# The first attention's values: who measures the rows, and one norm batch instead of three

## What is computed

```
h   = h + attention0(layernorm(h)) @ Wo
xn  = (h - mean(h)) / sqrt(var(h) + 1e-5)            # per row of 256
logits = xn @ router_w ; top 2 of 8 experts per row ; gate = softmax(top 2)
e_out  = layernorm(xn + W2 gelu(W1 xn + b1) + b2)    # each row by its 2 experts
h   = h + sum over the 2 experts of gate * e_out
h   = h + attention1(layernorm(h)) ; h = h + low_rank_ffn(layernorm(h))
```

## Time and profile before

| what | us |
|---|---|
| median of 3 runs (808.05 to 809.29) | 808.77 |
| the profiled execution's own time | 809.9 |
| its span, first to last instruction | 807.9 |
| busy: PE, PEld, DVE, POOL, ACT | 710.4, 608.9, 515.6, 423.8, 378.5 |
| PE's share of the chain that ended last | 74% |

### The profile page before, as it was taken

How to read it: one execution, slowest core, us unless ns; L and a number is a source line. 1 busy time by engine, 2 the same in 40 slices (tenths; PEclk the granted TensorE clock), 3 DMA queues, 4 the chain that set the end, 5 groups by cost and what they waited for, 6 DMA issues and landing times.

```text
span 807.9 us, 13117 instructions
## 1 busy us (share of the span) xinstructions
PE 710.4 (88%) x4247; PEld 608.9 (75%) x4247; DVE 515.6 (64%) x1230; ACT 378.5 (47%) x930; POOL 423.8 (52%) x360
## 2 busy tenths in 40 slices
PE   3669999999999999999847837999999999677797
PEld 3669998989889898655446736999999999444686
DVE  4567888778787787768988881223322233488957
ACT  3346666666576664643131332444444444156232
POOL 5555587676776853447949712343334432136640
PEclk9879999999999999999878967999999999689799
DMA  7943233323333202000011058898999992200001
GB/s 232 255 125 109 69 111 110 113 87 94 105 114 114 59 1 104 1 1 1 0 58 48 27 209 302 332 335 300 334 329 334 325 320 106 109 35 2 0 1 66
DMA packets 47064, 108.58 MB, mean 134 GB/s; under 512 B 5028, under 2 KB 24728, under 8 KB 39576
## 3 DMA queue, kind: packets, MB, share of 16 engines
q1 hardware_dynamic: 44408, 100.68, 37.3%
q0 software_dynamic: 2592, 7.10, 2.4%
HBM read 101.58 MB, written 6.17 MB: 133 GB/s over the span
## 4 chain that ended last, share of the span: by engine, by line
PE 74%; DVE 12%; SPq 3%; DMA 3%; POOL 3%; issue 2%; ACT 2%; DVEq 0%; ACTq 0%; POOLq 0%
PE banks L1703 12%; PE banks L1711 12%; PE banks L291 9%; PE banks L293 9%; PE banks L292 9%; PE banks L298 5%; PE banks L304 4%; PE banks L1311 3%; PE banks L1358 1%; DVE banks L1485 1%; PE banks L1285 1%; DVE a_o L1576 1%; DVE a_prod L1198 1%; PE banks L1341 1%; SPq L386 1%
## 5 line engine op out<-in xcount | busy, mean ns | idle before, releaser
L408 POOL TENSOR_TENSOR x_lo<-xraw,x_hi 128x512 fp32r<-128x512 f32 x81 | 105.6, 1304 | 99.7 <-ACT x_hi L402 99.6
L1794 ACT ACTIVATE hid<-banks,b 128x128 f32<-128x128 f32 x216 | 79.4, 368 | 110.4 <-PE banks L1703 110.4
L291 PE MATMUL banks<-wc_hi,x_hi 128*128 128x256 f32 x324 | 99.1, 306 | 19.4 <-POOL x_hi L411 13.3
L292 PE MATMUL banks<-wc_lo,x_hi 128*128 128x256 f32 x324 | 94.0, 290 | 0.0
L293 PE MATMUL banks<-wc_hi,x_lo 128*128 128x256 f32 x324 | 93.9, 290 | 0.0
L1959 DVE TENSOR_TENSOR res<-banks,xb 128x256 f32<-128x256 f32 x27 | 11.5, 425 | 127.3 <-PE banks L1711 127.3
L291 PEld LDWEIGHTS banks<-wc_hi,x_hi 128*128 128x128 f32 x324 | 64.3, 198 | 21.3 <-issue 13.5
L442 DVE BATCH_NORM_STATS2 stats<-banks 128x6 f32<-128x256 f32 x81 | 34.6, 428 | 69.4 <-ACT pe_sb L436 68.9
L291 PE MATMUL banks<-wkv_hi,xg_hi 128*128 128x512 f32 x162 | 70.9, 438 | 6.5 <-DVE xg_lo L503 6.3
L1832 POOL TENSOR_TENSOR y<-bve,mhalf 128x1 f32<-128x1 f32 x27 | 20.2, 747 | 105.7 <-DVE bve L1967 105.7
L402 ACT ACTIVATE x_hi<-xraw 128x768 fp32r<-128x768 f32 (+1 forms) x81 | 66.8, 830 | 12.1 <-DMA xraw<-in_x_rest 12.1
(11 more groups left out here) (331 smaller groups left out, 1828.1 us busy)
## 6 DMA issues: line engine op xcount, KB each, us to landing
w_raw<-in_w SPq DMA_DIRECT2D x28, 1024.0 KB, 6.6
xraw<-in_x_main SPq DMA_DIRECT2D x27, 768.0 KB
w1more<-in_w SPq DMA_DIRECT2D x13, 1024.0 KB, 6.0
w2more<-in_w SPq DMA_DIRECT2D x13, 1024.0 KB, 8.9
xraw<-in_x_rest SPq DMA_DIRECT2D x48, 96.0 KB
xraw<-in_x_rest SPq DMA_DIRECT2D x27, 114.0 KB
yl<-y_rows SPq DMA_DIRECT2D x2, 1028.0 KB, 6.9
a_w<-in_qkv_w SPq DMA_DIRECT2D x2, 768.0 KB, 5.4
```

The costliest lines, as they stand in the source:

```text
L291: pe.matmul(dst, a[0], b[0], start=start, stop=False)
L292: pe.matmul(dst, a[0], b[1], start=False, stop=False)
L408: pool.tensor_tensor(x_lo[:, i % RING_X, :], xraw[:, k, 0:KF].rearrange("p c b -> p (c b)"), x_hi[:, i % RING_X, 0:KF * P], ALU.subtract). ...
L1794: act.activation(hid[:, s % 2, fc, :], bank(fc % 2, 0, P), ACT.Gelu, bias=b1[:, bass.ds(e * FC + fc, 1)]).then_inc(sem("gelu_made"), 1)
```

## The change

ACT's copy of `h(t)` also accumulates the sum of the row (`accum_out`). A new `square_row(t)` on ACT, one turn behind, makes minus the mean with a one-element copy and then squares the row with that as its bias, accumulating the squared deviations; the squares themselves go to the place of `x2`, where they are overwritten later. DVE's `add_o` is left for layer 1 only. The three norm batches become one: `row_variances` (DVE, between the second and third `route_top`), one `pow` of ten elements a partition on POOL, `row_shifts` (DVE, behind the third `route_top` and ahead of the routing's chain). ACT writes all ten rows of `x2` behind it. `center_router` moves from ahead of DVE's second odd tile to behind the second half of the softmax, ahead of the third. All three `route_top` now stand in `dve_route`. One semaphore of a memset is merged into another.

```diff
 def copy_h(act, layer, t):
-    act.activation(h_at(t), bank(6 + t % 2), ACT.Copy).then_inc(sem("a_h_made"), 1)
+    act.activation(h_at(t), bank(6 + t % 2), ACT.Copy, accum_out=row_sum_of[:, layer, t:t + 1]).then_inc(sem("a_h_made"), 1)
+def square_row(act, t):
+    act.wait_ge(sem("a_h_made"), t + 1)
+    act.activation(mv[1][:, t, 0:1], row_sum_of[:, 0, t:t + 1], ACT.Copy, scale=-1.0 / C).then_inc(sem("row_measured"), 1)
+    act.wait_ge(sem("row_measured"), 2 * t + 1)
+    act.activation(x2[:, t * C:(t + 1) * C], h_at(t), ACT.Square, bias=mv[1][:, t, 0:1],
+                   accum_out=mv[1][:, t, 1:2]).then_inc(sem("row_measured"), 1)
...
 # act_attention, layer 0, turn t, behind copy_hT(t - 3)
-if layer == 0 and t == 7:
-    norm_rows(act, 0)
+if layer == 0 and t:
+    square_row(act, t - 1)
...
 copy_h(act, layer, T - 1)
 if layer == 0:
+    square_row(act, T - 1)
     for t in range(T - 3, T):
         copy_hT(act, t)
...
 # dve_attention
-if layer == 0 and i == 1:
+if layer == 0 and i == 2:
     center_router(dve)
...
+def row_variances(dve):
+    dve.wait_ge(sem("row_measured"), 2 * T)
+    dve.tensor_scalar(veps[1][:, :], mv[1][:, :, 1], 1.0 / C, 1e-5, ALU.mult, ALU.add).then_inc(sem("var_made"), 1)
+def row_shifts(dve):
+    n = batch_of("experts", 0)[0]
+    dve.wait_ge(sem("rstd_made"), n + 1)
+    dve.tensor_tensor(nmr[1][:, :], mv[1][:, :, 0], rstd[1][:, :], ALU.mult).then_inc(sem("nmr_made"), 1)
...
 # dve_route
-for a, b in GROUPS[1:]:
+for a, b in GROUPS:
     route_top(dve, link, a, b)
+    if b == T - 2:
+        row_variances(dve)
+row_shifts(dve)
 link(dve.tensor_copy(topf[:, :, :], topi[:, :, 0:2]))
...
-def norm_rows(act, group):
-    normalized_scales(act, "experts", group)
-    for t in range(*GROUPS[group]):
+def norm_rows(act):
+    normalized_scales(act, "experts")
+    for t in range(T):
         normalize(act, x2[:, t * C:(t + 1) * C], h_at(t), t, 1).then_inc(sem("x2_made"), 1)
```

More of the change, by code:

```diff
@@ L100, in vision_tower @@
         spare = sb("spare", [P, 2])
+        row_sum_of = sb("row_sum_of", [P, 2, T])
         rstd = [sb(f"rstd{i}", [P, T]) for i in range(3)]
@@ L319, in vision_tower @@
         SET = {"class": 1, "attention 0": 2, "experts": 1, "attention 1": 0, "low rank": 1}
-        BEFORE = {"class": 0, "attention 0": 0, "experts": 1, "attention 1": NW, "low rank": 2}
+        BEFORE = {"class": 0, "attention 0": 0, "attention 1": NW, "low rank": 1}
         BATCHES = [("attention 0", 0, NW - 2), ("attention 0", NW - 2, NW - 1), ("attention 0", NW - 1, NW), ("attention 0", NW, T),
-                   ("experts", 0, 4), ("experts", 4, 8), ("experts", 8, T), ("attention 1", 0, 2), ("attention 1", 2, 6), ("attention 1", 6, T),
+                   ("experts", 0, T), ("attention 1", 0, 2), ("attention 1", 2, 6), ("attention 1", 6, T),
                    ("low rank", 0, T - BT), ("low rank", T - BT, T)]
@@ L1269, in pool_attention @@
             if layer == 0:
-                for part in range(3):
-                    inverse_std(pool, *batch_of("experts", part))
+                inverse_std(pool, *batch_of("experts", 0))
             else:
@@ L1577, in dve_attention, with add_o @@
                    .then_inc(sem("a_o_made"), 1)
-                while added < t - 3:
-                    add_o(dve, layer, added)
+                while layer == 1 and added < t - 3:
+                    add_o(dve, added)
                     added += 1
[L1581 to L1593, removed]
+            if layer == 1:
+                for t in range(added, T):
+                    add_o(dve, t)
+        def row_variances(dve):
[5 more added lines that the diff above has]
+            dve.tensor_tensor(nmr[1][:, :], mv[1][:, :, 0], rstd[1][:, :], ALU.mult).then_inc(sem("nmr_made"), 1)
+        def add_o(dve, t):
+            dve.wait_ge(sem("a_h_made"), seen(1, "h_made", t + 1))
+            ends = {7: 0, T - 1: 1}
+            tile_stats(dve, "low rank", t, h_at(t))
             if t in ends:
-                add_eps(dve, following, ends[t])
-            if layer == 0 and t - 1 in ends:
-                shift_of(dve, *batch_of(following, ends[t - 1]))
+                add_eps(dve, "low rank", ends[t])
         def top_two(dve, link, x, t8, ti, tf, count):
@@ L1762, in sp_experts @@
                 load_weights(sp, s, s if s < E else sp.value_load(owner[0:1, s - E:s - E + 1], min_val=0, max_val=E - 1))
-        def norm_rows(act, group):
-            normalized_scales(act, "experts", group)
-            for t in range(*GROUPS[group]):
+        def norm_rows(act):
+            normalized_scales(act, "experts")
+            for t in range(T):
                 normalize(act, x2[:, t * C:(t + 1) * C], h_at(t), t, 1).then_inc(sem("x2_made"), 1)
         def act_experts(act):
-            norm_rows(act, 1)
-            norm_rows(act, 2)
+            norm_rows(act)
             act.wait_ge(sem("tw_made"), 1)
@@ L1807, in pool_route_constants @@
             pool.memset(not_first[:, :, :], 1.0).then_inc(sem("route_fill"), 1)
-            pool.wait_ge(sem("route_fill"), 2)
+            pool.wait_ge(sem("route_fill"), 3)
             pool.affine_select(out=before[:, :], in_=before[:, :], compare_op=ALU.is_gt, fill=0.0,
@@ L1868, in dve_route @@
                .then_inc(sem("route_ready"), 1)
-            shift_of(dve, *batch_of("experts", 2))
             link(dve.tensor_tensor(tw[:, :, :], top[:, :, 0:2], top[:, :, 0:1].broadcast_to([P, T, 2]), ALU.subtract))
@@ L2172, in _ @@
         def _(pool):
-            pool.memset(ident[:, :], 0.0).then_inc(sem("ident_zeroed"), 1)
+            pool.memset(ident[:, :], 0.0).then_inc(sem("route_fill"), 1)
             pool.memset(mhalf[:, :], -0.5).then_inc(sem("consts_made"), 1)
@@ L2176, in _ @@
             pool.memset(xraw[:, :, 4, :], 0.0).then_inc(sem("pads_zeroed"), 1)
-            pool.wait_ge(sem("ident_zeroed"), 1)
+            pool.wait_ge(sem("route_fill"), 1)
             pool.affine_select(out=ident[:, :], in_=ident[:, :], compare_op=ALU.not_equal, fill=1.0,
```

## The result

| | median us | lowest to highest | runs |
|---|---|---|---|
| before, measured beside it | 809.67 | 807.75 to 811.01 | 8 |
| changed | 811.55 | 809.88 to 812.08 | 8 |

The ratio is 1.0026, 95% interval 1.0015 to 1.0038. The changed kernel is slower, by 1.9 us between the medians and by 1.2 to 3.1 us by the interval. The profiled execution took 811.4 with a span of 809.7; before it was 809.9 and 807.9.

A forecast was written before the change was run, and what follows sets the result against it. POOL was taken to pace the values' stage, a PE-ACT zigzag to end it, then DVE's routing chain, and PE from 490 on. Terms -0.05 + 1.3 = +1.25 on 808.77 gave 810.0 us, range 807.8 to 811.8.

The forecast's parts named there:

- DVE's relief: Values' stage: 7.8 us less before DVE's last odd tile, ready near 452 instead of 460; worth nothing.
- ACT's turn: Values' stage: 1.1 us added per tile (read-outs 0.20, copy 0.20, square 0.51), hidden in ACT's idle time in turns 1 to 6.
- The end of the zigzag: End of the values' stage, between PE and ACT: gain spent on the last square; -0.05, bounds -0.3 and +0.5.
- the upper bound: Zigzag's end with a read-out of 0.4: +0.5, from three read-outs less 0.3 of slack, then two more.
- the first rival: Slower: ACT's read-out costs 0.6, hT(7) at 468.06, zigzag +1.25, kernel 811.3; chance 0.17.
- The norm batch: Routing on DVE: topf newly waits for POOL's ten-element pow, 471.72 instead of 470.44; +1.3, bounds 1.1 and 1.6.
- The rows of x2: Behind the shift: ACT's ten rows end at 476.8, SP's weight loads start 4 us later; all hidden, at nothing.
- the second: Faster rival: first gather meets no backlog, lands in 3.2, saves 3.4, kernel 806.7; chance 0.12, half of it a partial form.
- the third: Rival: third route_top's index search waits at the shared port until 471.56; +1.6, kernel 810.4; chance 0.05.
- The read-out of 0.6: The claim of the first rival: ACT's read-out costs more than an instruction; slower from 0.35; chance 0.17.
- DVE as the bound: Fourth rival, values' stage: DVE's end was the bound, -7.8 + 1.3, kernel 802.3; chance 0.03.
- The clock's rise: PE's rise to 2.4 GHz, first expert slot: 0.65 gained if it stays put, 0.65 lost if it comes as much later.

The follow-up runs named there:

- e4: Kernel before with one norm batch of ten rows, x2 written behind all copies, shift behind the scan, DVE still measuring every row; 0.9992 of before's time.
- e8: Changed kernel with the router centred ahead of DVE's second odd tile again and layer 1's copies of h not accumulating; one run, 811.15 us.
- e2: e1 with the last tile's square_row also moved, behind copy_hT(9) instead of ahead of copy_hT(7); 0.9988 of before's time.
- e1: Changed kernel with one line moved, row_shifts behind the routing's scan (rank) instead of ahead of topf; 1.0002 of before's time.
- e3: Changed kernel with the ten-element power done twice on POOL, first to a place nobody reads; 1.0025 of before's time.
- e5: e4 with the loads of b1, b2 and gamma issued ahead of the stores of x2; 0.9987 of before's time.

## Why the prediction was right, and where it was not

The time of 811.55 lies in the range, near its upper end of 811.8; 0.9 of its distance from the forecast 810.0 is that the kernel before, too, came out higher beside it (809.67 and not 808.77). The forecast, +1.25, is at the lower edge of the first interval, +1.2 to +3.1, and below the second, +1.6 to +3.7. I gave "within 0.2%" more chance than "slower", where 0.26% and 0.33% were measured. The mechanism was right and the sum too small.

**DVE's relief worth nothing: right.** e4 leaves every measurement on DVE, e8 undoes the centring, and PE takes DVE's last tile at the same place in both. In the changed kernel that tile is ready at 452.39 on the clock of before (452 forecast). POOL's folds and PE's order set it.

**ACT's turn: right.** Read-out 0.19 for 0.20, copy 0.20, square 0.51; nothing on the path in turns 1 to 6.

**The end of the zigzag: right in kind, -0.21 for -0.05.** `turn_h(8)` is 0.21 sooner. I had put `h(9)`'s read-out behind its copy and `copy_hT(7)` behind the last read-out; the trace has each overlap by 0.1. e2 shows the square's own price there, 0.84. The working of the upper bound does not add up: it names three read-outs ahead of `h(9)`, but the +0.5, and the 468.06 of the first rival, count two. With three the bound is +0.65. At the measured read-out of 0.19 nothing hangs on it.

**The norm batch: right.** `veps` at 469.29 on the clock of before (469.36 forecast), the power 1.97 (1.95), `topf` at 471.71 (471.72). The parts are right to 0.1; that the end is right to 0.01 is chance. Taken away in e1 and doubled in e3, the wait answered each time.

**The sum's missing parts.** Two terms stood nowhere. Layer 1's `copy_h` got the read-out as well, 0.1 at each of two places on the path: I priced the edit in layer 0 only, though the diff shows `layer` in its index. And from `topf` to `dst_row` 0.44 was added: PE's two rank products took 0.56 and 0.57, 0.36 and 0.37 before, with PE at its lower level (granted clock 0.50; 1.00 before). When I wrote down what e1 would show, I held a longer idle time of PE for the cause, but e4 has the same 2.36 of idle time as the kernel before and still 0.56 and 0.57. The rows of PE, before and in e4:
```profile
471.81 0.36 PE L1677 MATMUL banks<-rank,before 128*128 128x8 f32 x2 [2.36 <-DVE rank L1866]
```
```profile
471.06 0.56 PE L1672 MATMUL banks<-rank,before 128*128 128x8 f32 x2 [2.36 <-DVE rank L1860]
```
Of all the traces, only that of the kernel before has these products at the upper level. So 0.4 of the 1.71 may belong to that execution and not to the change; whether it does stays open, as there is one trace of it. Without it the terms give 1.5, with it 1.9.

**The rows of x2 hidden: right, but narrowly.** The loads began at 478.11, 4.0 later on a common clock, and the first gelu was not held. Gamma landed at 490.96 (480.26, its issue, plus 10.7), 2.6 ahead of the first gelu at 493.55, which is the cover forecast (491.4 against 494). But that cover does not carry over: in e1, with a chain shorter by 1.4, gamma was issued at the same place (480.33) and took 12.8, and the gelu waited for it. The gathers start 1.2 sooner there; that they delay gamma is likely and not shown.

**The rivals.** The gather landed after 6.63 in both traces, so the second never occurred, and with a shorter backlog in front (e5) it did not come sooner either. The index search took its usual 0.16 beside the power (469.31, while the power ran from 468.73 to 470.70), so the wait of the third did not occur. The read-out of 0.6 is excluded by the rows, and DVE as the bound by the place where PE takes its last tile. The clock's rise did move: it came 1.8 sooner behind the first turn and gave back 0.9 in the profiled pair, and it ranges from 4.4 to 9.6 behind the first turn over the traces; I had allowed 0.65.

## What to carry to other kernels

Merging small batches delays the first result to the last input: before merging, find who waits for the merged result and put its start, not its place of use, early enough. Work moved off an engine that the chain of waits names pays only if another engine's written order does not hold the next step anyway, and the engine that receives it may have its only critical moment exactly there. And price an edited helper at every caller.

## What the runs showed of the hardware

An ACTIVATE with an accumulated output is followed by a read of 0.19 us that the engine does as an instruction of its own; it overlaps its neighbours by about 0.1, and who waits for the instruction is released 0.1 later (0.48 and 0.38 in the chain of the changed kernel and of e8). A power of 128x10 took 1.97 on POOL, in line with 0.70 for two and 1.64 for eight. PE's rise to 2.4 GHz in the first expert slot came between 4.4 (after) and 9.6 us (e1) behind its first turn, and the 27 slots took 198.4 us in the first case and 201.5 in the second, which has the wait for gamma too.
